# Two buffers per gathered row slot in a relational graph layer's loop, and a rearranged way into it

## The reference, cut to what matters

```python
def _L1_gnn_ref(feat, weight, src, dst, etypes):      # weight: 16 x 64 x 64
    h_src = feat[src]
    msg = jnp.zeros((h_src.shape[0], weight.shape[2]))
    for r in range(num_rels):
        mask = etypes == r
        msg = msg + h_src * mask[:, None] @ weight[r]
    return jax.ops.segment_sum(msg, dst, num_segments=feat.shape[0])
```

## Time and profile before

| | us |
|---|---|
| median of three runs (lowest to highest) | 2144.19 (2142.64 to 2149.27) |
| the profiled execution | 2166.85 |
| its span from first to last instruction | 2165.1 |
| PE matmul busy | 1718.9 (79%) |
| DVE busy | 1494.2 (69%) |
| ACT busy | 1130.6 (52%) |
| POOL busy | 902.7 (42%) |
| relational loop, from 507 to 1411 | 904 |

### The profile page before, as it was taken

How to read it: one execution, slowest core, us unless ns; L and a number is a source line. 1 busy time by engine, 2 the same in 40 slices (tenths; PEclk the granted TensorE clock), 3 DMA queues, 4 the chain that set the end, 5 groups by cost and what they waited for, 6 DMA issues and landing times. The chain is left out here.

```text
span 2165.1 us, 36951 instructions
## 1 busy us (share of the span) xinstructions
PE 1718.9 (79%) x9927; PEld 872.9 (40%) x9928; DVE 1494.2 (69%) x4067; ACT 1130.6 (52%) x2244; POOL 902.7 (42%) x828
## 2 busy tenths in 40 slices
PE   2777776883588888888878888869998998899786
PEld 0222222551244433444434434455545453544254
DVE  6999997425466565665566656578886887788855
ACT  6777776212233333333333433338885887788521
POOL 1000000005666666666666666415553554455500
PEclk9999999996799999999998989979999999999898
DMA  6000000102111111111111111130000000000000
GB/s 175 0 0 0 0 0 8 66 1 63 31 32 29 30 30 29 29 30 31 30 33 30 29 29 30 31 97 1 1 1 1 1 1 1 1 1 1 15 1 16
DMA packets 29633, 50.74 MB, mean 23 GB/s; under 512 B 12820, under 2 KB 13826, under 8 KB 29054
## 3 DMA queue, kind: packets, MB, share of 16 engines
q0 software_dynamic: 17664, 18.12, 4.9%
q1 hardware_dynamic: 11890, 31.59, 4.7%
HBM read 36.58 MB, written 7.39 MB: 20 GB/s over the span
## 5 line engine op out<-in xcount | busy, mean ns | idle before, releaser
L943 POOL DMA_INDIRECT adj<-h_table,l_idx x544 | 559.2, 1028 | 315.8 <-issue 147.1
L1133 DVE TENSOR_SCALAR adj<-adj,node_key 125x1024 f16<-125x1024 f16 x825 | 374.1, 496 | 356.8 <-PE psum L1078 174.3
L1078 PE MATMUL psum<-adj,x_sb 125*128 125x512 f16 x1650 | 435.3, 403 | 160.7 <-DVE adj L1133 137.8
L1643 POOL TENSOR_TENSOR gat_ring<-gat_ring,adj 125x750 f32<-125x750 f32 (+2 forms) x225 | 311.3, 1385 | 263.8 <-ACT gat_ring L1697 261.7
L1538 DVE SCALAR_TENSOR_TENSOR gat_ring<-x_sb,gat_node,psum 125x750 f32<-125x750 f32 (+2 forms) x375 | 317.9, 861 | 60.8 <-PE psum L1774 26.4
L1006 ACT ACTIVATE l_z<-psum 128x320 f32<-128x320 f32 x204 | 89.2, 437 | 478.7 <-remote 258.6
L1078 PEld LDWEIGHTS psum<-adj,x_sb 125*128 125x128 f16 x1650 | 159.2, 102 | 371.5 <-DVE adj L1133 184.2
L393 PE MATMUL psum<-col_hot,src_hot 128*128 128x500 bf16 x808 | 205.7, 376 | 110.1 <-DVE src_hot L322 88.9
L1771 PE MATMUL psum<-gat_ring,gat_hx 125*65 125x500 f32 (+1 forms) x500 | 244.2, 578 | 17.8 <-DVE gat_ring L1549 9.5
L319 DVE TENSOR_SCALAR col_hot<-iota_h,c_tab 128x500 bf16<-128x500 f16 x808 | 227.7, 346 | 25.0 <-PE psum L393 20.5
L1694 ACT ACTIVATE gat_ring<-gat_ring,gat_node 125x750 f32<-125x750 f32 (+2 forms) x225 | 182.2, 810 | 61.0 <-DVE gat_ring L1538 59.1
(11 more groups left out here) (259 smaller groups left out, 2264.7 us busy)
## 6 DMA issues: line engine op xcount, KB each, us to landing
adj<-h_table,l_idx POOLq DMA_INDIRECT x544
adj<-key_table SPq DMA_DIRECT2D x33, 250.0 KB
adj<-adj SPq DMA_DIRECT2D x3, 1662.5 KB
adj_saved<-adj SPq DMA_DIRECT2D x1, 3840.3 KB
adj<-adj_saved SPq DMA_DIRECT2D x5, 688.2 KB
x_sb<-in_x SPq DMA_DIRECT2D x1, 781.2 KB
x_saved<-x_sb SPq DMA_DIRECT2D x1, 781.2 KB
out<-x_sb SPq DMA_DIRECT2D x5, 156.2 KB
```

What stands on the lines that cost most here:

```text
L943: pool.indirect_dma_start(out=to[:, t, :], out_offset=None, in_=table[:, :], in_offset=bass.IndirectOffsetOnAxis(ap=index[:, t:t + 1], axi ...
L1078: last = pe.matmul(psum[:, PAIR[half] + t, :], h_parts[:, k, :], select[0:P, k % SELECTS, t * GE:(t + 1) * GE], start=(k == 0), stop=(k == ...
L1133: v.tensor_scalar(select[0:P, k % SELECTS, :], keys, node_key[:, k:k + 1], None, ALU.is_equal).then_inc(s_sel, 1)
L1643: pool.tensor_tensor(slot, slot, adj[:, k, cols(c)], ALU.mult).then_inc(s["weight_ready"], 1)
```

## The change

Six things are changed.

1. `got`, the room for gathered rows, becomes two rooms, for even and odd turns; the second is a new allocation of 4 KB a partition. `s_got` becomes 2 x 4 semaphores. `fetch(j)` waits for z of turn j-2 instead of j-1; `fetch(1)` waits for no z.
2. To make the room, the edges' tables `d_tab` and `type_tab` live only during the build, packed in `tabs`. They are stored to DRAM at the start of the build, and loaded again at the start of the loop, ahead of the first keys, into the room of the hots, where DVE's chain of six (L1194 to L1199) works on them.
3. `add_residual` and the whole-array row sums (L862) are gone; `residual_and_sums` does both chunk by chunk within the last SAGE convolution.
4. ACT scales the relation weights behind the `h_parts` copies instead of ahead of them.
5. POOL starts the first eight gathers after one cast of indices; the two other casts follow them.
6. In the GAT's layer norm ACT makes an Exp of zero times the standard deviation behind the Sqrt.

```diff
-        d_tab = sb("d_tab", [128, G * GT], FP32, edge_scope)[:, :]
-        type_tab = sb("type_tab", [128, G * GT], FP16, edge_scope)[:, :]
+        tab_store = nc.dram_tensor("tab_store", [128, 3 * G * GT], FP16, kind="Internal").ap()
+        tabs = sb("edge_tabs", [128, 3 * G * GT], FP16, build_scope)[:, :]
+        d_tab, type_tab = tabs[:, 0:2 * G * GT].bitcast(FP32), tabs[:, 2 * G * GT:3 * G * GT]
...
                 def _(sp):
+                    sp.dma_start(tab_store, tabs).then_inc(s_tabs, 16)
                     for loaded in (s_mats, s_mats2, s_vecs, s_x):
                         sp.wait_ge(loaded, 16)
+                    sp.wait_ge(s_tabs, 16)
...
+            def residual_and_sums(link, tiles):
+                v, xc = nc.vector, x_sb[:, tiles, :]
+                link(v.tensor_tensor(xc, xc, z[:, tiles, :], ALU.add))
+                link(v.tensor_reduce(stat[:, 0, tiles], xc, AX.X, ALU.add))
+
             sage_layer("l0b", h[:, :, :], stack, high, parts, None, z[:, :, :], vec0("L0_b2"), mat("L0_W2l", 2 * D),
-                       False)
-            add_residual(nc, sem("l0_residual"), x_sb, z)
+                       False, after_chunk=residual_and_sums)
...
-        got = carve(4 * GT * 2 * D).rearrange("p (g t d) -> p g t d", g=4, t=GT)
+        got_odd = sb("l1_got_odd", [128, 4, GT, 2 * D], FP16, l1_scope)[:, :, :, :]
+        got = carve(4 * GT * 2 * D).rearrange("p (g t d) -> p g t d", g=4, t=GT), got_odd
...
-        dw_tab = hot_space.bitcast(FP32)[:, 0:G * GT]
+        loaded_tabs = hot_space[:, 0:3 * G * GT]
+        dw_tab, type_back = loaded_tabs[:, 0:2 * G * GT].bitcast(FP32), loaded_tabs[:, 2 * G * GT:3 * G * GT]
...
-                act.wait_ge(s_rel, 32)
-                act.activation(rel[D:2 * D, :, :], rel[D:2 * D, :, :], ACT.Copy, scale=1.0 / LO_SCALE).then_inc(s_relc, 1)
                 act.wait_ge(s_moved, 16)
                 for c, tiles in enumerate(chunks):
                     act.wait_ge(s_norm, c + 1)
                     act.activation(h_parts[:, tiles, 0:D], h[:, tiles, :], ACT.Copy).then_inc(s_hp, 1)
                     act.activation(tmp[:, tiles, :], h[:, tiles, :], ACT.Copy, scale=LO_SCALE).then_inc(s_hs, 1)
+                act.wait_ge(s_rel, 32)
+                act.activation(rel[D:2 * D, :, :], rel[D:2 * D, :, :], ACT.Copy, scale=1.0 / LO_SCALE).then_inc(s_relc, 1)
...
-                link(v.tensor_reduce(stat[:, 0, :], x_sb[:, :, :], AX.X, ALU.add))
...
-        s_got = [sem(f"l1_gathered{k}", l1_scope) for k in range(4)]
+        s_got = [[sem(f"l1_gathered{half}_{k}", l1_scope) for k in range(4)] for half in range(2)]
+        s_tabs_in = sem("l1_edge_tabs_in", l1_scope)
...
+                    sp.dma_start(loaded_tabs, tab_store).then_inc(s_tabs_in, 16)
                     keys(0, 0)
...
                         for k in range(4):
-                            pool.wait_ge(s_z, SIX * (j - 1) + FREED[k])
+                            if not static(j, 1):
+                                pool.wait_ge(s_z, SIX * (j - 2) + FREED[k])
                             pool.sem_inc(s_tick, 1)
-                            gather(got[:, k, :, :], idx[:, half, k * GT:(k + 1) * GT], s_got[k])
+                            gather(got[half][:, k, :, :], idx[:, half, k * GT:(k + 1) * GT], s_got[half][k])
...
                     pool.tensor_copy(idx[:, 0, :], src_tab[:, 0:4 * GT]).then_inc(s_ix0, 1)
+                    pool.wait_ge(s_ix0, 1)
+                    pool.sem_inc(s_tick, 1)
+                    for k in range(2):
+                        gather(got[0][:, k, :, :], idx[:, 0, k * GT:(k + 1) * GT], s_got[0][k])
                     pool.tensor_copy(idx_first[:, :], src_tab[:, 4 * GT:6 * GT]).then_inc(s_ix0, 1)
...
-                            pe.wait_ge(s_got[FETCHED[pos]], 16 * GT * (j + 1))
-                            rows = got[:, FETCHED[pos], :, :]
+                            pe.wait_ge(s_got[half][FETCHED[pos]], 8 * GT * (j + 2 - half))
+                            rows = got[half][:, FETCHED[pos], :, :]
...
-                    link(v.tensor_scalar(dw_tab, d_tab, pass_off[:, 0:1], None, ALU.subtract))
+                    dve.wait_ge(s_tabs_in, 16)
+                    link(v.tensor_scalar(dw_tab, dw_tab, pass_off[:, 0:1], None, ALU.subtract))
...
-                    link(v.scalar_tensor_tensor(dw_tab, dw_tab, 1.0, type_tab, ALU.add, ALU.add))
+                    link(v.scalar_tensor_tensor(dw_tab, dw_tab, 1.0, type_back, ALU.add, ALU.add))
...
-                              (nc.tensor, (*s_got, *s_first))):
+                              (nc.tensor, (*s_got[0], *s_got[1], *s_first, s_tabs_in))):
...
             act.activation(stat[:, 2, :], stat[:, 1, :], ACT.Sqrt).then_inc(s["ln_std"], 1)
+            act.wait_ge(s["ln_std"], 1)
+            act.activation(stat[:, 0, :], stat[:, 2, :], ACT.Exp, scale=0.0).then_inc(s["exp_begun"], 1)
```

More of the change, by code:

```diff
@@ L290, in gnn @@
         square = sb("square", [128, SETS, max(ACT_TILES), 128], FP16, build_scope)
-        s_bchain, s_hot, s_sq, s_src, s_used, s_outer, s_written = (sem(n, build_scope) for n in (
-            "build_chain", "col_hots_ready", "squares_ready", "src_hots_ready", "hots_used", "outer_done", "window_written"))
+        s_tabs, s_bchain, s_hot, s_sq, s_src, s_used, s_outer, s_written = (sem(n, build_scope) for n in (
+            "edge_tabs_stored", "build_chain", "col_hots_ready", "squares_ready", "src_hots_ready", "hots_used", "outer_done", "window_written"))
         passes = nc.values_load(npass[0:1, 0:1], min_val=1, max_val=N // W + 1)
@@ L408, in gnn @@
             nc.all_engine_barrier(sems_to_clear=None)
-            for s in (s_bchain, s_hot, s_sq, s_src, s_used, s_outer, s_written):
+            for s in (s_tabs, s_bchain, s_hot, s_sq, s_src, s_used, s_outer, s_written):
                 nc.sync.sem_clear(s)
@@ L959, in _ @@
                     pool.wait_ge(s_ix0, 3)
-                    pool.sem_inc(s_tick, 1)
-                    for k in range(2):
-                        gather(got[:, k, :, :], idx[:, 0, k * GT:(k + 1) * GT], s_got[k])
                     gather(pair_pick[:, 0, :, :], idx_first[:, 0:GT], s_first[0])
                     for k in range(2, 4):
-                        gather(got[:, k, :, :], idx[:, 0, k * GT:(k + 1) * GT], s_got[k])
+                        gather(got[0][:, k, :, :], idx[:, 0, k * GT:(k + 1) * GT], s_got[0][k])
                     gather(pair_pick[:, 1, :, :], idx_first[:, GT:2 * GT], s_first[1])
@@ L1039, in _, with z @@
                 def _(pe):
-                    def z(j, pos):
+                    def z(j, pos, half):
                         n = SIX * j + pos
@@ L1093, in turn @@
                         for pos, lo, hi in ((0, 0, 4), (1, 4, 8), (2, 8, 12), (3, 12, 18), (4, 18, 22), (5, 22, NT)):
-                            z(j, pos)
+                            z(j, pos, half)
                             if not static(j, LAST):
@@ L1347, in attention @@
     chunks = [slice(c * TC, (c + 1) * TC) for c in range(NC)]
-    names = ("agg_transposed", "x_added", "vecs_in", "x_kept", "ln_chain", "ln_centred", "ln_squared", "ln_var", "ln_std", "ln_chunk",
+    names = ("agg_transposed", "x_added", "vecs_in", "x_kept", "ln_chain", "ln_centred", "ln_squared", "ln_var", "ln_std", "exp_begun", "ln_chunk",
              "self_loops", "w_chain", "w_columns", "w_rows", "constants", "transposed", "transpose_copied", "first_projected",
@@ L1834, in _ @@
                 project(first + GC - 1)
-def add_residual(nc, s_res, x_sb, z, width=D):
-    with nc.Block() as block:
-        @block.vector
-        def _(dve):
-            nc.vector.tensor_tensor(x_sb[:, :, :], x_sb[:, :, :], z[:, :, 0:width], ALU.add).then_inc(s_res, 1)
-            dve.wait_ge(s_res, 1)
 def kernel(**inputs):
```

## The result

The changed kernel takes 2435.4 us (median of four, 2426.0 to 2440.1) against 2145.6 (2142.6 to 2149.3, also of four) for the kernel before: 1.132 times as long, 95% interval 1.1285 to 1.1355. It is 290 us slower, beyond the forecast's range and beyond its rival "dense", which was priced at 2255 and reached to 2270.

The account below looks back on a forecast made before the run. PE was taken as busiest (600 of 728 us), its signals held beside POOL's gathers. -17 + 8 - 4.4 - 0.35 + 0.4 - 1.3 = -14.7 us off the median 2144.19 gave 2129.5; own range 2112 to 2147, overall 2070 to 2225.

Parts of the forecast that it names:

- dense: Relational loop: rival that one stream of 16 lets PE's signals through once a turn; 2151 to 2270 us, chance 0.32.
- remote: Relational loop: ACT's copy of z waits 252.5 us, 51 times, read as PE's signals not passing POOL's gathers.
- The sign of it: Whole kernel: whether the change makes it slower, given 0.32, against faster 0.50 and same 0.18.
- the hold: Relational loop: PE's semaphore posts do not get through while POOL issues indirect gathers; a z copy came 19 us late.
- The slow bound: Relational loop: stream of 16 hurts as that of 36 did; 21.3 + 8.2 = 29.5 us a turn, +3.5.
- The forecast of 25.4: Relational loop: turns of 25.4 us, taken between 25.05 and 25.96; -0.55 x 31 = -17 us.
- the two turns with streams of 12: Relational loop of the kernel before: index copies 21.88 and 28.23 us apart, mean 25.05, used to price the new turn.
- Start-up: Start of the loop: first stream grows from 36 to 40 gathers, one of 16 follows; +8 us, bounds 5 and 18.
- Way in: Before the loop: residual, reduction and weight scaling leave the path, -4.4 us; first gather needs one cast, -0.35.
- Tables: Start of the loop: loading the tables from DRAM hides behind turn 0's gathers; 0, at worst +5 us.
- GAT: GAT layer norm: table load of 1.28 us moves to ACT's idle time behind the Sqrt; -1.28, at worst 0.
- the terms came to -5.6: Outside the second buffer and start-up: -4.4 and -0.35 on entry, +0.4 for semaphores, -1.3 for the GAT table load.

Follow-up runs that it names:

- e2: Changed kernel with both rooms, but POOL's old waits for z of turn j-1 put back: 2160.0 us, 0.9956 of the kernel before.
- e3: Changed kernel with POOL waiting behind each turn's first three slots for the rows just asked for: 2216.2 us, 1.0208 of the kernel before.
- e11: Changed kernel with a small memset and a wait for it behind each slot of gathers: 2141.5 us, 0.9898 of the kernel before.
- e1: Changed kernel with one room for gathered rows and the old waits, rest of the change kept: 2159.4 us, 0.9946 of the kernel before.
- e6: Changed kernel with POOL writing memsets from turn 1 on instead of gathering: 2113.1 us, 0.97 of the kernel before.
- e9: Changed kernel with each indirect gather replaced by two plain half-width transfers, 32 a turn: 1931.6 us, 0.89 of the kernel before.
- e13: Changed kernel with a small memset and its wait behind gathers 8 and 16: 2403.3 us, 1.1097 of the kernel before.
- e4: Changed kernel with POOL waiting once a turn, behind the eighth gather, for rows just asked for: 2227.9 us, 1.0277 of the kernel before.
- e15: Changed kernel with two memsets and their waits behind gathers 5, 10 and 16, on another chip: 2111.0 us, 1.0424 of the kernel before.
- e16: Changed kernel with a small memset and wait behind each slot, on a chip where the kernel before takes 2024.2 us: 2124.9 us, 1.0499.

## Why the prediction was wrong

**What held.** Gathers were not late and are not now (3.7 and 2.8 us). The 16 gathers became one stream, of 20.0 us and not 21.3, since one takes 0.95 when nothing disturbs it. The index copy released it. The reading of "remote" as PE's signals held beside a stream of gathers was right, and e2, e3 and e11 show it by bringing breaks back. It was read too strictly: some signals come through within a stream (ACT at 667.93), late. The sign of it was weighed at 0.32 against 0.68, and that was too little.

**The step that failed: the price of a turn under the hold, and the choice between its bounds.** The slow bound put PE's pace in a held stretch at 8.23 / 23 of full and the work behind the stream at 8.2 us, 29.5 in all. On the measured turn (692.70 - 658.66 = 34.04) two things were off in it, and a third in what was made of it.
- Busy time was counted as progress. In the held rest of the stream PE was busy 4.84 us, almost the 4.5 worked out, but this was 15 matmuls of 119 in the turn, at a clock of 0.71. The earlier trace rows had it in the brackets: 30 matmuls in 23 us against 46 in 8.7 is a quarter of the pace and not 0.36. So 53 of 119 matmuls were left and not 8.2 / 21.4 of them: 9.5 us at the pace of before, +1.3 (an estimate, since the matmuls are of several sizes).
- Nothing was put down for the way back. Behind the last gather it took 2.80 us (678.61 to 681.41) until ACT read, and then PE ran its 53 matmuls at a clock of 0.77 in 11.3 us, 4.7 a us instead of 51 in 7.5: +2.8 and, over the 9.5, +1.8. The clock had fallen to 0.50 by 674, after PE had stood idle from 666.4 to 671.2, and so the hold was paid for a second time: over the steady loop it is 0.81 instead of 0.93. 20.0 + 2.8 + 11.3 is 34.1, which is the bound's 29.5 with these terms and a stream 1.3 shorter.
- The next stream waits for position 4 of the turn. So what PE owes behind the stream cannot lie under the next one; POOL stands 14 us. The slow bound was built on this, stream and rest one after the other. The forecast of 25.4 was not: it went 4.1 us below the bound, about as much as the bound itself was short.

The forecast took 25.4 from the two turns with streams of 12. There the mean of 25.05 came from two turns with streams of 12, 12 and 8 and pauses of 2.1 to 2.5 us between them. They were not "nearest to a row with long streams and no start-up in it" either: they stand close behind the first stream of 36, and from 700 to 1300 us the streams of the kernel before are of 4 and 8, with 1.6 and 2.3 us (medians) behind them. A row with one piece of the new pattern is no price for a turn made of nothing else. It saw the hold in the kernel before, but counted the breaks at the slots as POOL's loss; they were what kept PE going. The forecast's own range has a slip too: from its terms, turns of 25.0 to 25.96 and a start-up of 5 to 18, it comes to 2114 to 2156.5 and not 2112 to 2147. The result lies far outside both.

**Start-up.** Taken at +8, bounds 5 and 18. The index copy of turn 0 now comes at 541.3 instead of 558.0, that of turn 1 at 596.8 instead of 585.8: +11.0, and with the way in taken off +16.7. Within the bounds.

**Way in.** The first gather comes at 502.94 instead of 508.68, -5.7 against -4.75 predicted, though e1, with the same way in, has it at 504.10, so some 1 us of it may be this execution's alone. The timelines of POOL, DVE and ACT, as in the earlier trace rows:

```profile
484.93 2.71 POOL L867 MEMSET l_aggT<- 64x3146 f32 x1 [471.95 <-POOLq L509]
...
502.94 1.30 POOL L956 DMA_INDIRECT adj<-h_table,l_idx  x1 [0.94 <-POOL l_idx L970]
```

```profile
484.98 2.71 DVE L874 TENSOR_SCALAR stat<-stat 125x25 f32<-125x25 f32 x1 [0.52 <-PEq L509]
...
505.74 0.67 DVE L1210 TENSOR_SCALAR adj<-adj,pass_off 128x816 f32<-128x816 f32 x1 [3.57 <-DMA adj<-tab_store]
...
510.30 0.58 DVE L1215 TENSOR_SCALAR adj<-adj 128x816 f32<-128x816 f32 x1
```

```profile
493.88 0.47 ACT L859 ACTIVATE x_sb<-adj 125x320 f16<-125x320 f32 x1 [0.96 <-DVE adj L889]
```

The `h_parts` copies begin 5.5 us earlier (4.4 predicted); they wait for the norm and not for the save of x. A part of the gain went where nobody had looked: the mean, a DVE instruction on 25 columns, took 2.71 us, exactly as long as POOL's memset that began 0.05 us ahead of it, and it had taken 0.86 behind the reduction before, by the timeline, again ending with that memset (487.49 + 2.71 = 490.20, the mean at 490.25). A like instruction on the same columns takes 0.18 a little later (L883). So most of the removed reduction had lain beside the memset. The Trainium skill says in "SBUF — State Buffer", on who interferes with whom, that a tensor_scalar of DVE in a two-port mode and GpSimd lock each other out for a whole instruction, and whoever issues first wins; the ends of the two instructions agree to 0.1 us in both traces, but which mode DVE was in no row shows.

**Tables.** Their load makes DVE wait 3.57 us, its chain ends 3.6 us later within the block, and z of turn 0 still waits for its gathers: nothing on the path, as predicted.

**GAT.** The Exp behind the Sqrt now pulls the table load in; timeline of ACT, as in the earlier trace rows. ACT has 0.95 us left ahead of the next copy instead of 2.08. From the last block of the loop's outputs to the end of the kernel -1.4 us, where -1.3 was predicted for this and +0.4 for the semaphores.

```profile
1686.46 1.28 ACT L1689 ACT_TABLE_LOAD   x1
...
1688.93 1.26 ACT L1694 ACTIVATE gat_hT<-psum 64x625 f32<-64x625 f32 x2 [0.95 <-PE psum L1735]
```

All but the second buffer together gain 11.7 us (8 to 16) by e1, where the terms came to -5.6. The entry (4.6 in e1, by its first gather) and the GAT (1.4) account for some 6 of it; where the rest is from was not looked for.

**What stays open.** Why indirect gathers hold PE's signals, which part of them does, and why some signals come through within a stream; why one chip of those used doesn't have it; how long a break must be by the length and number of the streams; and what the change is worth where there is no hold.

## What to carry to other kernels

A wait can be what keeps another engine going. Before taking waits away from an engine that issues gathers, look whether the "remote" waits of the others end with its pauses, and price the pattern without pauses by a row that has none. In a held stretch count instructions beside busy time, and look at the clock behind it. And where a stage's release hangs on the work that it delays, the two add up: write the turn as a chain before taking a mean.

## What the runs showed of the hardware

- Beside an unbroken stream of indirect gathers on POOL, PE's semaphore signals reach others late: PE's turned rows, done at 665.89, were read at 681.41, 2.80 us behind the last of 16 gathers, and a z in the kernel before 1.5 us behind the last of 36. Some come within the stream, late as well: a z done at 662.85 was read at 667.93, 9.3 us into a stream that ran on to 678.61. For the first 7.5 us PE was not slowed (51 matmuls), then it did 15 in 12.6 us.
- Neither a POOL that was busy 600 of 600 us with memsets (e6) nor 32 plain transfers in 17.9 us from POOL (e9) did this. The turns were 24.70 and 19.59 us instead of 34.65, with no "remote" wait.
- How much is held depends on the breaks: breaks of 1.08 us behind every 4 gathers gave turns of 25.13 us (e11), of 1.06 behind every 8 33.90 (e13), and one of 2.3 between two eights 28.35 (e4).
- On one chip of those used no wait was "remote" (e15, e16; e11, the same kernel as e16, has 136.0 us of ACT's z copy waits on another chip), and the kernel before took 2024 us there instead of 2141 to 2169.
- PE's granted clock fell to 0.50, 1.2 GHz, within a held stretch, behind 4.8 us without a matmul, and stayed there until 684 us, 2.6 us into the work that followed: 0.77 over those 14 us, 0.81 over the loop, where e9's was 0.98.
